# Expert routing image by image, through a table in DRAM, in a one-core vision layer

## The reference, cut to what matters

```
h = embed(x) + pos                                # 8 x 1024 x 256
h = h + attention(layernorm(h))                   # 8 heads of 32, a sigmoid gate, a final projection
# experts, on n = layernorm(h), for all 8192 tokens
H      = gelu(n @ W1 + b1)                        # 8192 x 1024
probs  = softmax(H @ Wg + bg)                     # 8192 x 8
assign = argmax(probs)
y      = probs[assign] * (H @ Wd[assign] + bd[assign])
out    = h + y
```

## Time and profile before

| what | value |
|---|---|
| median of 3 runs | 1827.46 us (1826.95 to 1827.72) |
| profiled execution, its time | 1824.39 us |
| its span, first to last instruction | 1822.6 us |
| mean granted TensorE clock | 0.967 |
| busy: PE, DVE, ACT, POOL | 1631.2, 1201.0, 943.0, 307.8 us |
| DMA moved | 187.57 MB |

### The profile page before, as it was taken

One profiled execution on the slowest core, in us unless ns is written; L12 is line 12 of the kernel. 1 busy time (PEld: TensorE's weight loads), 2 busy tenths in 40 slices (PEclk: granted clock), 3 DMA queues, 4 the chain that ended last, 5 costly groups with the idle time before them and its releaser, 6 DMA issues.

```text
span 1822.6 us, 29454 instructions
## 1 busy us (share of the span) xinstructions
PE 1631.2 (90%) x11124; PEld 1125.0 (62%) x11124; DVE 1201.0 (66%) x1904; ACT 943.0 (52%) x1560; POOL 307.8 (17%) x231
## 2 busy tenths in 40 slices
PE   8796999999999999999999999998885707999998
PEld 6463556556646665665657456645443506999998
DVE  2376686868777776777677767776666496444443
ACT  0465655756575657567565756575663331222222
POOL 0202000200200020002001000200000081555554
PEclk9798999999999999999999999999999858999999
DMA  4313235242604251342325141603330462666663
GB/s 162 87 53 69 43 94 132 57 99 64 144 19 111 68 147 23 106 117 81 87 67 131 42 110 53 162 5 89 80 83 20 118 163 90 199 202 204 208 198 129
DMA packets 121218, 187.57 MB, mean 103 GB/s; under 512 B 11883, under 2 KB 86265, under 8 KB 120956
## 3 DMA queue, kind: packets, MB, share of 16 engines
q1 hardware_dynamic: 104652, 120.42, 26.7%
q0 software_dynamic: 16000, 63.98, 10.9%
q10 hardware_dynamic: 432, 1.31, 0.2%
HBM read 84.98 MB, written 51.38 MB: 75 GB/s over the span
## 4 chain that ended last, share of the span: by engine, by line
PE 68%; DVE 18%; issue 7%; ACT 5%; DMA 1%; SPq 1%; POOL 0%; POOLq 0%; DVEq 0%; ACTq 0%
PE ps L509 12%; PE ps L752 11%; PE ps L523 11%; PE ps L476 8%; DVE nmax L1066 6%; ACT pr L854 3%; PE ps L740 3%; PE ps L559 3%; PE ps L536 3%; PE ps L497 3%; PE ps L580 2%; PE ps L582 2%; PE ps L581 2%; PE ps L543 1%; PE ps L450 1%
## 5 line engine op out<-in xcount | busy, mean ns | idle before, releaser
L1066 DVE TENSOR_REDUCE nmax<-ps 128x1 f32<-128x1024 f32 x512 | 623.7, 1221 | 216.7 <-PE ps L509 209.8
L854 ACT ACTIVATE pr<-ps,nmax 128x1024 f32<-128x1024 f32 x512 | 570.7, 1115 | 287.1 <-DVE nmax L1066 282.2
L509 PE MATMUL ps<-st 96*128 96x512 f32 x1024 | 399.6, 474 | 70.5 <-ACT pr L854 60.8
L509 PEld LDWEIGHTS ps<-st 96*128 96x128 f32 x1024 | 168.2, 191 | 266.5 <-ACT pr L854 128.6
L523 PE MATMUL ps<-pr,vs 128*32 128x256 f32 x4096 | 271.7, 386 | 11.5 <-DVE vs L957 11.5
L752 PE MATMUL ps<-wd,hg 128*128 x1728 | 224.9, 287 | 0.0
L752 PEld LDWEIGHTS ps<-wd,hg 128*128 128x128 f32 x1728 | 212.2, 192 | 0.0
L523 PEld LDWEIGHTS ps<-pr,vs 128*32 128x32 f32 x4096 | 108.8, 109 | 153.4 <-issue 70.4
L890 ACT ACTIVATE hg<-ps 128x512 fp32r<-128x512 f32 x144 | 78.6, 596 | 239.6 <-PE ps L740 234.8
L476 PE MATMUL ps<-wp,xt 128*128 128x256 f32 x672 | 172.8, 378 | 0.0
L823 ACT ACTIVATE ht<-ps,bf 128x512 f32<-128x512 f32 x128 | 88.3, 690 | 129.8 <-PE ps L582 129.8
(11 more groups left out here) (129 smaller groups left out, 1885.6 us busy)
## 6 DMA issues: line engine op xcount, KB each, us to landing
st<-qk SPq DMA_DIRECT2D x192, 256.0 KB, 5.1
xt<-x_in SPq DMA_DIRECT2D x58, 384.0 KB, 3.1
token_rows<-staged_b SPq DMA_DIRECT2D x64, 256.0 KB, 4.1
token_rows<-staged_a SPq DMA_DIRECT2D x64, 256.0 KB, 4.1
token_rows<-hres POOLq DMA_DIRECT2D x8, 1024.0 KB, 5.2
wd_raw<-w_down SPq DMA_DIRECT2D x64, 128.0 KB, 3.0
pr<-x_in SPq DMA_DIRECT2D x6, 384.0 KB, 9.0
rows<-token_rows,slot_from POOLq DMA_INDIRECT x72
```

Of the source, the lines that this page charges most:

```text
L509: last = mm(ps[:, 2 * (k % SR) + j, :], stq[:, hh, i * P:(i + 1) * P], stk[:, hh, j * 512:(j + 1) * 512], start=True, stop=True)
L854: actv(pr[:, k % PR, :], ps[:, 2 * (k % SR):2 * (k % SR) + 2, :].rearrange("p a n -> p (a n)"), ACT.Exp, bias=nmax[:, k % 16:k % 16 + 1], ...
L1066: V.reduce_max(nmax[:, k % 16:k % 16 + 1], ps[:, 2 * (k % SR):2 * (k % SR) + 2, :].rearrange("p a n -> p (a n)"), AX_X, negate=True).then_ ...
```

## The change: what it does

- Routing is done for each image inside the score steps of the image after it (`route`, `ROUTE_AT`, steps 36 to 51 on DVE; `prefix` on PE at step 47; `exponentials` on ACT at step 43). It keeps, for each expert, a running count `base`; a token's address in its expert's list is count plus its rank in the image.
- POOL writes the token's number to that address of a DRAM tensor `slot_table` by eight indirect DMAs an image, one a tile (`place`). The probability goes to four extra columns of the token's row (`store_prob`, one DMA of SP an image), so a row of `token_rows` is 5136 bytes in place of 5120.
- After the last image its own routing runs, then one indirect DMA reads the 72 rows of the table that are in use, PE turns them, and DVE makes `slot_from` and `slot_to`. The scans, the one-hot matmuls and their operands are gone.
- The experts' weights load from step 46 of the last image on. ACT rounds pieces 0 to 3 at steps 44, 48, 52 and 56, pieces 4 to 8 before the last router, pieces 9 to 15 between its Gelus. The raw buffers lie in the place of the last expert's weights. SBUF is laid out anew for it.
- 71 slots in place of 72.

```
+        DOWN_AT = {G_STEPS + 12 + 4 * m: m for m in range(4)}
...
# SP
+            def load_down(m):
+                i = m % WD_BUFFERS
+                wait(sp, "wd_low", m + 1 - WD_BUFFERS)
+                piece = w_down[m].rearrange("(i n) k d -> k n i d", n=BLK)
+                for k in range(P // BLK):
+                    sp.dma_start(wd_raw[k * BLK:(k + 1) * BLK, i], piece[k]).then_inc(wd_in[i], 16)
...
                 if before:
                     for u in range(4):
                         store_hidden(b - 1, u)
+                    store_prob(b - 1)
 
             over_images(sp, image)
...
+            sp.wait_ge(S["emb_mm"], IMAGES * TILES)
+            sp.dma_start(bd_raw, b_down).then_inc(S["bd_raw_in"], 16)
+            sp.wait_ge(S["h_sum"], IMAGES)
+            sp.wait_ge(S["g_mm"], 4 * IMAGES)
+            for m in range(8):
+                load_down(m)
+            load_down(8)
+            load_down(9)
+            store_hidden(IMAGES - 1, 0)
+            load_down(10)
+            load_down(11)
+            store_hidden(IMAGES - 1, 1)
+            load_down(12)
+            load_down(13)
+            store_hidden(IMAGES - 1, 2)
+            load_down(14)
+            load_down(15)
+            store_hidden(IMAGES - 1, 3)
+            store_prob(IMAGES - 1)
...
# POOL
+            def place(b):
+                wait(pool, "table_in", 16)
+                wait(pool, "addr_ready", b + 1)
+                for t in range(TILES):
+                    nc.gpsimd.indirect_dma_start(
+                        table_flat, bass.IndirectOffsetOnAxis(addr_i[:, t:t + 1], 0),
+                        tid[:, b * TILES + t:b * TILES + t + 1], None,
+                        bounds_check=EXPERTS * ALL_TILES * P - 1, oob_is_err=False).then_inc(S["table_out"], 16)
...
                 if after:
                     front(b + 1, 1 - par)
+                if before:
+                    place(b - 1)
 
             over_images(pool, image)
+            for m in range(4):
+                split_down(m)
             root_3(IMAGES - 1)
             store_rear(IMAGES - 1, (IMAGES - 1) % 2)
 
             pool.wait_ge(S["bd_high"], 1)
+            nc.gpsimd.tensor_tensor(bd_parts[:, 1], bd_raw, bd_parts[:, 0].bitcast(F32), ALU.subtract
+                                    ).then_inc(S["bd_low"], 1)
+            for m in range(4, WD_PIECES):
+                split_down(m)
+            pool.wait_ge(S["ff_mm"], 16 * IMAGES)
             nc.gpsimd.memset(bd[:].bitcast(F32), 0.0).then_inc(S["bd_zero"], 1)
...
# PE
+            def prefix(r):
+                wait(pe, "r_oh", r + 1)
+                mm(spare(0)[:, 0:(TILES + 1) * EXPERTS], up[:], oh[:, GUARD:].rearrange("p t e -> p (t e)"),
+                   start=True, stop=False)
+                mm(spare(0)[:, 0:(TILES + 1) * EXPERTS], ones[:].bitcast(F32),
+                   run[:, 2, GUARD:].rearrange("p t e -> p (t e)"), start=False, stop=True).then_inc(S["r_mm"], 1)
...
                     if after and k in QK0_AT:
                         j, c = QK0_AT[k]
                         if j == 0 and c == 0:
                             wait(pe, "tr_read", b * 8 + 16)
+                            wait(pe, "r_read", b)
...
# ACT
+            def high_down(m):
...
+                i = m % WD_BUFFERS
+                wait(act, wd_in[i], (m // WD_BUFFERS + 1) * 16 * (P // BLK))
+                actv(wd_piece(0, m), wd_raw[:, i], ACT.Identity).then_inc(S["wd_high"], 1)
...
                         actv(ht[:, k, :], spare(bank), ACT.Gelu, bias=bf1[:, k:k + 1]).then_inc(S["ff_act"], 1)
+                        if b == IMAGES - 1 and k % 2 == 1 and HC * hf + k < 14:
+                            high_down(9 + (HC * hf + k) // 2)
...
+                    if before and k == PREFIX_AT - 4:
+                        exponentials(b - 1)
+                    if not after and k in DOWN_AT:
+                        high_down(DOWN_AT[k])
...
             over_images(act, image)
+            act.wait_ge(S["bd_raw_in"], 16)
+            actv(bd_parts[:, 0], bd_raw, ACT.Identity).then_inc(S["bd_high"], 1)
+            for m in range(4, 9):
+                high_down(m)
             router(IMAGES - 1)
...
# DVE: route(r, i), 14 numbered pieces of one or two instructions on 64 or 72 columns; i = 9 gives prob_ready,
# i = 10 reads the prefix (r_read), i = 13 gives addr_ready
+            ROUTE_AT = {G_STEPS + 4: (0, 1), G_STEPS + 5: (2,), G_STEPS + 6: (3,), G_STEPS + 7: (4,), G_STEPS + 8: (5,),
+                        G_STEPS + 9: (6,), G_STEPS + 10: (7,), G_STEPS + 13: (8,), G_STEPS + 14: (9,),
+                        PREFIX_AT + 1: (10,), PREFIX_AT + 2: (11,), PREFIX_AT + 3: (12,), PREFIX_AT + 4: (13,)}
```

More of the change, by code:

```diff
@@ L42 @@
 SLOTS = ALL_TILES + EXPERTS
-ROW = HID + D
+ROW = HID + D + 4
+PROB = HID + D
+USED = SLOTS - 1
+GUARD = 4
 RING = 6
@@ L686, in image @@
                         turn(b + 1, TURN_AT[k])
+                    if before and k == PREFIX_AT:
+                        if after:
+                            wait(pe, "tr_read", b * 8 + 15)
+                        else:
+                            wait(pe, "g_tanh", b * 4 + 3)
+                        prefix(b - 1)
                     if after and k in QK0_AT:
@@ L705, in _ @@
             turn_logits(IMAGES - 1, 1, 1)
-            pe.wait_ge(S["r_oh"], 1)
-            oh_flat = oh[:].rearrange("p t e -> p (t e)")
-            mm(ps[:, 0, :], up[:], oh_flat, start=True, stop=True)
-            mm(ps[:, 1, :], ones[:].bitcast(F32), oh_flat, start=True, stop=True).then_inc(S["r_mm"], 1)
-            def sort(j, first, last):
-                for i in range(2):
-                    wait(pe, "val_ready", j * 2 + i + 1)
-                    for t in range(8):
-                        done = mm(ps[:, 2, 0:2 * SLOTS], row_hot[:, i, t, :], slot_val[:, i, t],
-                                  start=(first and i == 0 and t == 0), stop=(last and i == 1 and t == 7),
-                                  skip_group_check=True)
-                    done.then_inc(S["sort_mm"], 1)
-            SORT_PAIRS = ALL_TILES // 16
-            sort(0, True, False)
-            with pe.Fori(1, SORT_PAIRS - 1) as j:
-                sort(j, False, False)
-            sort(SORT_PAIRS - 1, False, True)
+            wait(pe, "lg_done", 2 * IMAGES)
+            prefix(IMAGES - 1)
+            pe.wait_ge(S["tab_in"], 16)
+            nc.tensor.transpose(ps[:, 2, 0:SLOTS], tab, ident[0:SLOTS, 0:SLOTS]).then_inc(S["tab_mm"], 1)
             pe.wait_ge(S["slots_ready"], 1)
+            pe.wait_ge(S["slots_in"], 1)
             pe.wait_ge(S["bd_in"], 16 * 2 * EXPERTS)
@@ L838, in image @@
                     wait(act, "fin_mm", b * 4)
+                if not before:
+                    wait(act, "table_in", 16)
                 for hf in range(2):
@@ L1074, in image @@
                         scale_v(b, SCALE_AT[k])
+                    if before and k in ROUTE_AT:
+                        for i in ROUTE_AT[k]:
+                            route(b - 1, i)
                     if before and k in NORM_AT:
@@ L1169, in _ @@
-            over_pairs(dve, ALL_TILES // 16, select)
-            for e in range(EXPERTS):
-                link(V.scalar_tensor_tensor(slot_f[:, (e + 1) % 2, :], sst[:], cnt[:, 1, e:e + 1], slot_f[:, e % 2, :],
+            last = IMAGES - 1
+            for i in range(8):
+                route(last, i)
+            for i in (10, 11, 12, 13):
+                route(last, i)
+            for i in (8, 9):
+                route(last, i)
+            final_base = base[:, IMAGES % 2, :]
+            wait(dve, "r_read", IMAGES)
```

376 lines of the change are left out of this document (207 added, 169 removed).

## The result

The changed kernel takes 1849.45 us (median of 4 runs, 1847.19 to 1851.56), the kernel before 1827.2 beside it (4 runs, 1818.61 to 1827.72): ratio 1.0133, 95% interval 1.0099 to 1.0166. It is slower by 1.3%, and outside the forecast range of 1806 to 1837. In a later set of runs the same two kernels stood at 1869.57 and 1823.95: 1.0249 (1.0228 to 1.0270).

The account below looks back on a forecast made before the run. PE was taken to bound images and experts, with an 84.3 us gap after the last logits; terms -3.9 - 58.0 + 8.5 + 13.6 + 5.2 + 29 + 0.5 = -5.1 gave a median of 1822.4 us, range 1806 to 1837.

Parts of the forecast that it names:

- The slot: Experts: 72 slots become 71, at 3.87 us a slot, -3.9 us.
- End of the routing: Last logits to first turned rows: 26.3 us in place of 84.3, -58.0 (-59 to -53 by the landings taken).
- The routed images: Seven images: routing mostly hidden in gaps, about 1.2 us an image, +8.5 in all; 37 if all exposed.
- PE's wait for `r_read`: Each routed image, `project` at step 49: DVE's read comes late, so PE waits 0.7 us.
- a sign of being wrong: Routed images: the prediction is wrong if an image grows by more than 2.5 us.
- The last image: Late first weight piece, slowed clock, three more roundings and POOL's low parts: +13.6 us (9 to 18).
- The clock behind the stop: Last image: PE idles while ACT waits for the first weight piece, its clock falls; taken as 2.0 us.
- the value scaling behind four low parts: Last image: POOL's four low parts block DVE instructions with SBUF sources, the value scaling among them, 1.5 us.
- Before the last router: Rounding of piece 8 ahead of the Gelus waits for its buffer and load, delaying ACT: +5.2 us.
- Inside the last router: ACT waits for pieces 10, 12, 14, loaded behind stores: PE stands 23 us, plus 2.0 clock each, +29 (20 to 31).
- Unaligned rows: Rows of 5136 bytes slow stores of H: possibly +6.6 us, taken as nothing; as a rival, sum +1.5, 1829, chance 0.12.
- slower, routing exposed: Rival: DVE's routing pieces delay the images, 3.5 us an image, 25 us: +11, 1839; chance 0.18.

Follow-up runs that it names:

- e9: e7 without GpSimd's eight scatters in each of images 0 to 6, those tokens missing from the table: 1790.55 us, ratio 0.9808 to the kernel before.
- e7: Changed kernel with weight loads one store earlier, low parts after norm 3, piece 8 behind the first Gelu, first roundings later: 1817.66 us, ratio 0.9951.
- e12: The changed kernel itself, with no edit, run again beside the kernel before in a later set: 1869.57 us, ratio 1.0249.
- e3: Changed kernel with ACT's roundings of pieces 0 to 3 at steps 53, 56, 59, 62 of the last image: 1834.7 us, ratio 1.0053.
- e1: Changed kernel with each pair of weight pieces loaded one store of H earlier on SP's queue: 1823.85 us, ratio 0.9994 to the kernel before.
- e4: Kernel before with rows of 5136 bytes and one small store an image into the new columns: 1828.85 us, ratio 1.0019.

## Why the prediction was wrong

It named the right places and the right sign for each, and went wrong in sizes, all on one side. The terms measured sum to +27.2 against -5.1.

- **The slot:** -3.5 for -3.9. Right.
- **End of the routing:** -53.1 for -58.0. The mechanism held. The term that was mis-sized is the landing of the scattered words: 2.0 taken, but from the end of the last issue (1549.00) to the gather of the table (1556.33) it took 7.3. The case bounded it at 4.2; the nearest rows were of plain DMAs.
- **The routed images:** +14.0 for +7.8, and here two steps failed. `place` got no price in the images at all. And PE's wait for `r_read` was priced at its 0.7 alone: it came in each image at 0.6, but in images 2, 3 and 6 of the first profile the clock was at 0.50 for 3.4 us behind it, which the text counted for the last image and not here. Images 4 and 5, without this, grew by 1.2 and 0.6, as forecast; images 1, 3 and 6 by 3.6 to 4.0, past the 2.5 that the text had named as a sign of being wrong. Without scatters 10.2 is left (e9), so in the first profile they cost some 4 at most; in the sets with holes they are the larger part, 27.2 and 28.8 in all (e7, e12), and they cost 9 in e7's last image.
- **The last image:** +21.9 for +14.8. Exponential 45 started some 10 us late for 8.3, since the first piece took 5.8 from issue to rounding, not 4.2. The clock behind the stop was priced at 2.0, but PE ran at 0.50 for ten us (1386 to 1396). And the value scaling behind four low parts, priced at 1.5, took 3.93 in place of 0.29 and left PE idle 3.75. With the roundings moved behind the loads (e3) the stretch was 163.6; how the 16.9 that went divide between wait, clock and the later roundings isn't separated.
- **Before the last router:** +12.6 for +5.2. The failed step is that low parts on POOL were held against DVE instructions in the image only, and not against norm 3, which reads and writes SBUF, stood beside five low parts, and lost 12.6 us. The wait for piece 8, which was priced, ended at 1453.49, ahead of the norm's end at 1459.95 (1444.39 + 15.56), and cost nothing by itself.
- **Inside the last router:** +35.3 for +29. The mechanism is shown by e1 (31 us). The term that was mis-sized is the load: from the first issue of a pair of loads to the rounding took 6.8, where a load alone had landed in 4.2 and 5.2 was taken; the four stores took 3.4 to issue for 2.8. So PE stood 10.64 and 9.59 us in the first two stops, for 8.4 and 6.2.
- **Unaligned rows:** left out at nothing. The stores land 0.5 to 0.7 later, and e4's +3.5 in the whole time can't be put on the rows.
- **The rivals:** "slower, routing exposed" was right in direction (1839), and that was luck: images 4 and 5 show the arithmetic nearly hidden, as forecast. No rival held the scatters as a load on the other queues, and the one-sided errors, 5 to 7 us in each of five terms, add: a queue behind a queue, a clock behind a stop.

## What to carry to other kernels

An indirect DMA that scatters single words is not free because its engine is idle: price its issue (1.27 us each here), the time until its words have landed, and what other queues lose meanwhile, and keep it away from loads that something waits for. A load whose buffer is released by the engine that also waits for it needs to be issued ahead of any store which depends on that engine's next result; three edits of order turned +1.3% (in another set +2.5%) into -0.5%. When a wait is short but on the engine that bounds the stretch, allow for the clock behind it. When work is moved under other work, list what each moved instruction shares (SBUF port, queue, clock) with each of its new neighbours, since stalls of this kind add.

## What the runs showed of the hardware

- A VectorE `TENSOR_SCALAR` from SBUF to SBUF of 128 x 256 elements, 0.40 us alone, took 13.3 us once beside a row of GpSimd `TENSOR_TENSOR`s; it lasted until the whole row had ended, not one of them.
- Eight indirect DMAs of 128 four-byte words from GpSimd went with a hole of 2.5 us or more in each image on two chips, with a hole in one image on a third, and with 15.3 us on a fourth where loads stood behind them; as many words as plain DMAs of SyncE, to consecutive addresses, made no hole.
- One-row DMAs of SyncE landed after 1.7 us (median) without such scatters and after 6.0 beside them.
- The same program cost 1.33% more than the kernel before in one set of runs and 2.49% in another, far apart beside either interval. The profiles put most of the difference where the scatters run.
- A wait of PE of only 0.6 us came in each of six images of the changed kernel, and in three of them the granted clock was at 0.50 for 3.4 us behind it. Behind an idle time of 2.09 us it fell in e4_pitch and not in the kernel before.
